# Last layer: sums over slots and the product with adj on VectorE in the gathered buffer, one matmul a block

## What is computed

```python
s = node_feats @ msg_w[:, :D].T
d = node_feats @ msg_w[:, D:].T
messages = gelu(s[:, None, :] + d[None, :, :] + msg_b)
aggregated = einsum('ijd,ij->id', messages, adj)
new_feats = concatenate([node_feats, aggregated]) @ upd_w.T + upd_b
h = gelu(new_feats) + node_feats
return layernorm(h) * ln_w + ln_b
```

## Time and profile before

| | |
|---|---|
| median of three runs | 939.18 us (938.51 to 940.09) |
| the profiled execution, its own time | 940.4 us |
| its span, first to last instruction | 938.7 us |
| TensorE (PE) busy | 685.3 us, 73% |
| GpSimd (POOL) busy | 517.7 us, 55% |
| VectorE (DVE) busy | 426.3 us, 45% |
| ScalarE (ACT) busy | 365.3 us, 39% |

### The profile page before, as it was taken

The page is one execution under the profiler, slowest core; times in us unless marked ns, Lnnn a source line. Parts: engine busy times, 40 slices in busy tenths (PEclk is TensorE's granted clock), DMA queues, the critical chain, the costliest instruction groups (busy, mean ns, idle before and its releaser), DMA issues.

```text
span 938.7 us, 8329 instructions
## 1 busy us (share of the span) xinstructions
PE 685.3 (73%) x2458; PEld 402.5 (43%) x2458; DVE 426.3 (45%) x1529; ACT 365.3 (39%) x591; POOL 517.7 (55%) x513
## 2 busy tenths in 40 slices
PE   1254666999799997989466985285777588589794
PEld 1211142444365644535355633063455356355463
DVE  2298837098986398914435200204413333143222
ACT  0456623468314239654301240134234324442541
POOL 7999199876762067620270067574746656657200
PEclk8669555999879998979655577577979979788685
DMA  8976801799651039930120011111211112111000
GB/s 355 362 283 282 364 1 59 269 409 383 234 186 60 1 133 403 397 150 21 48 60 26 26 40 50 40 50 35 55 32 43 48 37 49 46 45 40 16 6 5
DMA packets 35041, 120.80 MB, mean 129 GB/s; under 512 B 9014, under 2 KB 21748, under 8 KB 25972
## 3 DMA queue, kind: packets, MB, share of 16 engines
...
HBM read 114.66 MB, written 5.55 MB: 128 GB/s over the span
## 4 chain that ended last, share of the span: by engine, by line
PE 44%; DVE 12%; another core or an unknown queue 11%; issue 10%; POOL 8%; DMA 8%; ACT 7%; SPq 0%; POOLq 0%; ACTq 0%
PE ps L114 43%; POOL X L924 8%; DMA ring<-in_adjT_dram 8%; ACT dg L1149 2%; DVE Mh L1744 1%; DVE M L1733 1%; ACT L1158 1%; ACT msg L1158 1%; DVE st L1772 1%; DVE w L1617 1%; DVE w L1619 1%; PE ps L1282 1%; DVE Mh L1732 1%; DVE w L1615 1%
## 5 line engine op out<-in xcount | busy, mean ns | idle before, releaser
L913 POOL DMA_INDIRECT G<-near,IX x176 | 176.5, 1003 | 124.2 <-issue 52.4
L924 POOL TENSOR_TENSOR X<-X,ring 128x2708 f32<-128x2708 f32 (+1 forms) x22 | 129.8, 5902 | 25.9 <-DMA ring<-in_adjT_dram 23.1
L114 PE MATMUL ps<-ring,xT_s 128*128 128x512 f32 (+2 forms) x264 | 114.0, 575 | 8.6 <-DMA ring<-in_adjT_dram 8.6
L114 PE MATMUL ps<-ring,hwu 128*128 128x512 f32 (+3 forms) x264 | 117.0, 597 | 1.0 <-ACT hwu L1016 1.0
L1740 DVE COPY listed<-ps 128x386 f32<-128x386 f32 x11 | 6.2, 560 | 238.6 <-issue 85.6
L114 PE MATMUL ps<-G,ident 128*128 128x512 f32 (+1 forms) x88 | 57.9, 743 | 51.3 <-ACT msg L1158 43.5
L1551 DVE FIND_INDEX8 I<-V,rows 128x8 uint32<-128x340 f32 (+2 forms) x176 | 88.1, 504 | 0.0
L1561 DVE MAX8 V<-rows 128x8 f32<-128x340 f32 (+2 forms) x176 | 85.6, 497 | 0.8
L114 PEld LDWEIGHTS ps<-ring,hwu 128*128 128x128 f32 (+1 forms) x264 | 52.0, 207 | 65.9 <-issue 64.6
L114 PE MATMUL ps<-pd,ident 128*128 128x512 f32 (+3 forms) x116 | 70.1, 701 | 6.9 <-issue 4.9
L1023 ACT ACTIVATE binT<-ring 128x2708 bf16<-128x2708 f32 (+1 forms) x22 | 54.0, 2456 | 44.2 <-PE ps L114 36.0
...
## 6 DMA issues: line engine op xcount, KB each, us to landing
...
G<-near,IX POOLq DMA_INDIRECT x176
...
```

Source lines behind the costliest of these rows:

```text
L114: return pe.matmul(dst, lhsT, rhs, start=start, stop=stop, skip_group_check=True)
L913: pool.indirect_dma_start(out=dst, out_offset=None, in_=table, in_offset=bass.IndirectOffsetOnAxis(ap=index, axis=0), bounds_check=N - 1, ...
L924: pool.tensor_tensor(S[0:rn(j), 0:N], S[0:rn(j), 0:N], ring[0:rn(j), j % RING, :], ALU.add).then_inc(o_S, 1)
```

## The change

- The group loop makes only d. s follows behind the loop for six chunks of four blocks; own_parts on VectorE adds msg_b and writes pd3.
- before_gelu(n) is on VectorE, in G3: it adds s, which own_shares puts in PSUM by an identity product, to the eight slots, and to d of the block itself as a ninth slot. messages(n) takes the gelu of all nine in place. aggregate(n) on VectorE multiplies the nine by T9 (T8 with diag as ninth column) and sums over them; TensorE then adds the block by one identity product that also transposes it. weights and messages_own are gone.
- take_list reads the three groups with six operations instead of ten.
- G3 has room for six blocks; a place is free when VectorE has aggregated its block. A pair's list is gathered before its blocks.
- The gathers have no bound. With it the built program has a register write of 2707 ahead of each of the 231 gathers; without it none.
- lists(1) stands ahead of the group loop, rows_to_list(2) behind it; normal2(0) comes before take_list(1); checks() moves behind pair 1.

The diff, cut to its core:

```diff
-QUEUE3 = 4
+QUEUE3 = 6
...
-        T8 = sb("T8", [P, NB, TOP])
+
+        T9 = sb("T9", [P, NB, TOP + 1])
+        T8, diag = T9[:, :, 0:TOP], T9[:, :, TOP]
...
-        G3 = sb("G3", [P, QUEUE3, TOP, D], life=life)
+        G3 = sb("G3", [P, QUEUE3, TOP + 1, D], life=life)
...
-                                        in_offset=bass.IndirectOffsetOnAxis(ap=index, axis=0),
-                                        bounds_check=N - 1, oob_is_err=False).then_inc(signal, 16)
+                                        in_offset=bass.IndirectOffsetOnAxis(ap=index, axis=0)).then_inc(signal, 16)
...
             for g in range(NG3):
-                for n in (2 * g, 2 * g + 1):
-                    if n >= QUEUE3:
-                        pool.wait_ge(p_pre, 2 * (n - QUEUE3 + 1))
-                    for k in range(TOP):
-                        gather(G3[0:rn(n), n % QUEUE3, k, :], near3[:, :], IX[0:rn(n), n, k:k + 1], s_g[2 * (n % QUEUE3) + k // 4])
                 pool.wait_ge(v_list, g + 1)
                 if g >= 2:
                     pool.wait_ge(p_opre, g - 1)
                 for k in range(CAP):
                     gather(Go[:, g % 2, k, :], near3[:, :], IO[:, g, k:k + 1], s_go[g % 2])
+                for n in (2 * g, 2 * g + 1):
+                    if n >= QUEUE3:
+                        pool.wait_ge(v_agg, n - QUEUE3 + 1)
+                    for k in range(TOP):
+                        gather(G3[0:rn(n), n % QUEUE3, k, :], near3[:, :], IX[0:rn(n), n, k:k + 1], s_g[n % QUEUE3])
...
             def messages(n):
-                r = rn(n)
-                if n >= 2:
-                    act.wait_ge(p_agg, n - 1)
-                for h in range(2):
-                    act.wait_ge(p_pre, 2 * n + h + 1)
-                    act.activation(msg[0:r, n % 2, 4 * h:4 * h + 4, :], bank((2 * n + h) % 3)[0:r, :].rearrange("p (k d) -> p k d", d=D),
-                                   ACT.Gelu).then_inc(c_msg, 1)
+                act.wait_ge(v_pre, n + 1)
+                at = G3[0:rn(n), n % QUEUE3, :, :]
+                act.activation(at, at, ACT.Gelu).then_inc(c_msg, 1)
...
-            def update(g):
-                act.wait_ge(p_sums, g + 1)
...
+            def features(g):
...
+            def deviations3(g):
...
-            weights(0)
-            for q in range(CH):
-                messages_own(q)
-            weights(1)
             for g in range(NG3):
+                messages_listed(g)
                 messages(2 * g)
                 if g:
-                    weights(2 * g + 1)
-                    messages_listed(g - 1)
-                    update(g - 1)
+                    deviations3(g - 1)
                 messages(2 * g + 1)
-                if 2 * g + 2 < NB:
-                    weights(2 * g + 2)
-            messages_listed(NG3 - 1)
-            update(NG3 - 1)
+                aggregated(g)
+                features(g)
+            deviations3(NG3 - 1)
...
                 if g == 0:
                     pe.wait_ge(c_pr, CH)
                     lists(0)
-                if g == 1:
                     lists(1)
...
+            for q in range(CH):
+                if q >= 2:
+                    pe.wait_ge(v_s, q - 1)
+                for i, n in enumerate(blocks_of(q)):
+                    last = mm(pe, bank(6 + q % 2, i * D, D)[0:rn(n), :], x3T[:, n, 0:rn(n)], w3c[:, D:2 * D], True, True)
+                last.then_inc(p_pr, 1)
+
+            def own_shares(g):
+
                 if g >= 2:
-                    pe.wait_ge(c_pr, CH + g - 1)
-                for q, n in enumerate(range(first, first + count)):
-                    at = bank(4 + g % 2, q * D, D)[0:rn(n), :]
...
-                    last = mm(pe, at, ones[0:1, 0:rn(n)], b3_b[0:1, 0:D], False, True)
+                    pe.wait_ge(v_pre, 2 * g - 2)
+                if g < NG3 - 1:
+                    last = mm(pe, bank(g % 2, 0, 2 * D), ident[:, :], pd3[:, 2 * g:2 * g + 2, D:2 * D], True, True)
+                else:
...
+                        n = 2 * g + i
+                        last = mm(pe, bank(g % 2, i * D, D)[0:rn(n), :], ident[0:rn(n), 0:rn(n)], pd3[0:rn(n), n, D:2 * D], True, True)
                 last.then_inc(p_pr, 1)
...
-            def before_gelu(n):
-                r = rn(n)
-                for h in range(2):
-                    if 2 * n + h >= 3:
-                        pe.wait_ge(c_msg, 2 * n + h - 2)
-                    pe.wait_ge(s_g[2 * (n % QUEUE3) + h], past2[2 * (n % QUEUE3) + h] + 64 * (n // QUEUE3 + 1))
-                    at = bank((2 * n + h) % 3)[0:r, :].rearrange("p (k d) -> p k d", d=D)
-                    mm(pe, at, ident[0:r, 0:r], G3[0:r, n % QUEUE3, 4 * h:4 * h + 4, :], True, False)
-                    last = mm(pe, at, ident[0:r, 0:r], pd3[0:r, n, D:2 * D].unsqueeze(1).broadcast_to([r, 4, D]), False, True)
-                    last.then_inc(p_pre, 1)
...
-            def aggregate(n):
...
-                for k in range(TOP):
-                    mm(pe, at, msg[0:r, n % 2, k, :], dg[0:r, n % 2, k, 0:r], n % 2 == 0 and k == 0, False)
-                mm(pe, at, msgd[0:r, n, :], dg[0:r, n % 2, TOP, 0:r], False, False).then_inc(p_agg, 1)
...
+                    pe.wait_ge(c_aggS, g)
...
+            def aggregate(n):
+                r = rn(n)
+                pe.wait_ge(v_agg, n + 1)
+                mm(pe, bank(5, n % 2 * P, r), agg[0:r, n % 2, :], ident[0:r, 0:r], False, n % 2 == 1).then_inc(p_agg, 1)
...
+            pe.wait_ge(v_s, CH)
+            pe.wait_ge(c_d, len(GROUPS2))
+            own_shares(0)
+            own_shares(1)
             for g in range(NG3):
-                before_gelu(2 * g)
-                if g:
-                    aggregate(2 * g - 1)
-                    listed_before_gelu(g - 1)
-                    aggregate_listed(g - 1)
-                    new_features(g - 1)
+                listed_before_gelu(g)
                 if g + 2 < NG3:
                     lists(g + 2)
-                before_gelu(2 * g + 1)
+                aggregate_listed(g)
                 aggregate(2 * g)
-            aggregate(NB - 1)
-            listed_before_gelu(NG3 - 1)
-            aggregate_listed(NG3 - 1)
-            new_features(NG3 - 1)
+                aggregate(2 * g + 1)
+                if g + 2 < NG3:
+                    own_shares(g + 2)
+                new_features(g)
...
-                dve.tensor_copy(listed[:, 0:2, :], bank(7, 0, 2 * EDGE).rearrange("p (k e) -> p k e", e=EDGE))
-                few.done(dve.tensor_copy(listed[:, 2, :], bank(6, 0, EDGE)))
-                for k in range(CAP):
-                    for i, (to, of) in enumerate(((eidx[:, k:k + 1], listed[:, k, 0:w]), (eval_[:, g, k:k + 1], listed[:, k, w:2 * w]))):
-                        dve.scalar_tensor_tensor(out=Mh[:, i, k * w:(k + 1) * w], in0=listed[:, k, 2 * w:3 * w], scalar=ecol[:, k:k + 1], in1=of,
-                                                 op0=ALU.is_equal, op1=ALU.mult, accum_out=to)
+                here, chosen = Mh[:, 0, 0:CAP * w].rearrange("p (k w) -> p k w", w=w), Mh[:, 1, :].rearrange("p (k i w) -> p k i w", i=2, w=w)
+                few.done(dve.tensor_copy(listed[:, :, :], list_bank[:, :, 0:EDGE]))
+                few.done(dve.tensor_tensor(here, listed[:, :, 2 * w:3 * w], ecol[:, :].unsqueeze(2).broadcast_to([P, CAP, w]), ALU.is_equal))
+                few.done(dve.tensor_tensor(chosen, listed[:, :, 0:2 * w].rearrange("p k (i w) -> p k i w", w=w),
+                                           here.unsqueeze(2).broadcast_to([P, CAP, 2, w]), ALU.mult))
+                few.done(dve.tensor_reduce(entry[:, g, :, :], chosen, AX.X, ALU.add))
                 few.done(dve.tensor_copy(erow[:, g, :], listed[:, :, 3 * w]))
-                dve.tensor_copy(IO[:, g, :], eidx[:, :]).then_inc(v_list, 1)
+                dve.tensor_copy(IO[:, g, :], entry[:, g, :, 0]).then_inc(v_list, 1)
...
             for g, (first, count) in enumerate(GROUPS2):
+                normal2(g, first, count)
                 if g == 0:
-                    rows_to_list(2)
-                if g == 1:
                     take_list(1)
-                normal2(g, first, count)
...
+            def own_parts(q):
+
...
+                dve.wait_ge(p_pr, CH + q + 1)
...
+                    last = dve.tensor_tensor(pd3[0:r, n, D:2 * D], bank(6 + q % 2, (first - b[0]) * D, m * D)[0:r, :].rearrange(
+                        "p (q w) -> p q w", w=D), b3_b[0:r, 0:D].unsqueeze(1).broadcast_to([r, m, D]), ALU.add)
+                last.then_inc(v_s, 1)
...
+            def before_gelu(n):
+                r, q = rn(n), n % QUEUE3
+                own = bank(n // 2 % 2, n % 2 * D, D)[0:r, :]
+                dve.wait_ge(p_pr, 2 * CH + n // 2 + 1)
+                dve.tensor_tensor(G3[0:r, q, TOP, :], pd3[0:r, n, 0:D], own, ALU.add)
+                dve.wait_ge(s_g[q], past2[q] + 128 * (n // QUEUE3 + 1))
```

(36 more changed lines are left out.)

91 lines of the change are left out of this document (25 added, 66 removed).

## The result

The changed kernel took 957.2 us (median of four runs, 955.8 to 960.0) against 939.6 for the kernel before: ratio 1.019, 95% interval 1.017 to 1.022. I had forecast 808 us with 0.03 for slower. The profiled execution has a span of 955.2 us. Ratios in this document leave out runs in the slower state of the chip, of which c1_after (823.0 us) and d1_before_group (864.8 us) have one each, so they are not always the quotient of the medians beside them.

The account below looks back on a forecast made before the run. TensorE's own order was taken as the bound. First pair aggregated at 544.8, ten pairs at 24.4, 2 for checks() and a 16.6 tail gave a span of 807.4, so 808 us; range 772 to 836.

Parts of the forecast that it names:

- What bounds the kernel: Last layer's pair loop: TensorE in its own order, with ScalarE's messages between its steps, takes 31.4 us a pair.
- the way round in a pair: Last layer after the change: the chain through VectorE, TensorE and ScalarE sets each pair, 24.4 us at half clock.
- T + 4.6: Pair loop: TensorE ends new_features 4.6 us after VectorE ends aggregating the pair's second block.
- T + 9.0: Pair loop: TensorE ends the listed sums 9.0 us after VectorE ends aggregating the pair's second block.
- Group loop: Ahead of the last layer: each further group of four costs 6.05 us instead of 9.3; first gather 515.7 instead of 543.4.
- My middle: Gathers without the bound: 1.15 us each, taken between 1.00 (whole gap goes) and 1.30 (nothing gained).
- The lock-out by VectorE's product: Pair loop: a gather beside VectorE's product of two SBUF inputs waits; 0.7 us a block, 1.4 a pair.
- The reduction: VectorE's strided sum over a block's 1152 elements: 1.35 us, with bounds 1.35 and, at half rate, 2.7.
- my two cases: TensorE's clock in the pair loop: half clock, 24.4 us a pair (taken), or full clock, 20.2.
- 0.75 and more wherever wide products stand: TensorE's granted clock, argued for the rival of full clock and cheap gathers: 760 to 790 us, chance 0.19.
- the rival in which the bound was free and gathers decide: Last layer: gathers stay at 1.30 us, 24.8 a pair; kernel 813 us, up to 830; chance 0.18.
- the one rival for that, VectorE locking out gathers: Pair loop: busy VectorE locks out each gather; 939 us reached at 37 us a pair, 1.96 a gather; chance 0.03.

Follow-up runs that it names:

- c1_after: The changed kernel itself, nothing altered, in a session where the kernel before takes about 860 us: 814.4 us, ratio 0.938.
- d1_before_group: The kernel before with only the new group loop (second projection behind it, list steps moved): first gather at 518.3, only 8 us gained at the end.
- d4_before_look: The kernel before, nothing altered, run for its trace in a session where it takes about 860 us instead of about 940.
- d2_reduce_in_line: The changed kernel with the reduction reading its elements in the order they lie, without the stride: 814 us, a reduction 1352 ns instead of 2086.
- e2_half_gathers: The changed kernel with only four of eight gathers a block from the seventh block on: 23.9 us a pair; no kernel time given.
- f2: The changed kernel with 400 small DMAs added and GpSimd waiting for TensorE's listed sums ahead of each pair's block gathers: 871 us.
- f1: The changed kernel with 400 small DMAs from SyncE added in the pair loop, without any added GpSimd wait: 952 us.
- h1: The changed kernel with added GpSimd waits for TensorE in both layers' gathers, and three more in the first two pairs: 855.9 us.
- h2: The changed kernel itself, nothing altered, measured again in the session of the kernel with most added waits: 949.8 us.
- g3_before_pause: The kernel before with GpSimd waiting, ahead of each pair's block gathers, until TensorE has added up block 2g-3: 939.0 us.

## Why the prediction was wrong

**What bounds the kernel.** I took all of the 31.4 us a pair for TensorE's work in its own order, because it was busy 76%. In d4_before_look the same order takes 27.3. The mechanism was right for the most part, and 4 of the 31.4 us were something else: on record TensorE was busy 23.9 us a pair at a granted clock of 0.82, where d4_before_look has 20.8 at 0.89 (667.12 to 816.69, with 552 matmuls recorded instead of 576), and ScalarE waited 7.9 to 8.6 us "remote" ahead of `dg` in every second pair, where d4_before_look has 2.4 to 2.5 ended by TensorE. The sign was in the earlier trace rows: 43.5 and 24.8 us of ScalarE that end "remote". I read only idle times with a named releaser. Not every such wait is a sign, though: VectorE waits 16.6 us a pair for its list in d4_before_look as well, there with TensorE named.

**The step that failed** is the way round in a pair, 24.4 us. There ScalarE copies new_features at T + 4.6 and takes the listed sums at T + 9.0, as soon as TensorE has made them. On record, in the pair shown, it copied new_features 4.9 us and took the listed sums 23.5 us after TensorE's records of them end, every second pair was held up in this way, and a pair took 36.3 us on average. Against c1_after, where nothing is late, the first gather came 10.8 us later, the gathers took 362.9 us instead of 267.7, and from the last gather to the end it was 63.9 us instead of 28.4.

**Group loop.** The 6.05 us a group were 6.11 in c1_after (copies of `x3T` there start at 489.32 and 495.43), the first gather 517.6 against 515.7. On record it was 528.4, 10.8 later than in c1_after, where the two idle times together are 12.3 us shorter.

**Gathers.** 1.25 us, not 1.15: leaving out the bound shortened the instruction by 0.05, and the 0.30 gap did not go. My middle was wrong, the upper bound nearly right. The lock-out by VectorE's product is real but was over-sized. Two products of c1_after, and three gathers beside them:

```profile
682.55 1.36 DVE L1787 TENSOR_TENSOR G<-G,T 128x1152 f32<-128x1152 f32 x1 [0.50 <-ACT G L1124]
707.11 1.34 DVE L1787 TENSOR_TENSOR G<-G,T 128x1152 f32<-128x1152 f32 x1
```
```profile
682.71 2.02 POOL L910 DMA_INDIRECT G<-near,IX  x1 [0.30 <-issue]
706.59 0.94 POOL L910 DMA_INDIRECT G<-near,IX  x1 [0.30 <-issue]
707.84 1.43 POOL L910 DMA_INDIRECT G<-near,IX  x1 [0.30 <-issue]
```

The gathers that start inside a product, at 682.71 and 707.84, both end 2.2 us after the product's start, as if they had begun about when it ended; so do all 19 of c1_after that start between 0.1 and 1.2 us into a product (2.1 to 2.2). But most start just before a product or in its last 0.3 us, where it costs them 0.1 us or nothing. So of all 176 block gathers on record the mean is 969 against a median of 947 ns, 0.4 us a pair and not 1.4. The Trainium skill (SBUF — State Buffer, Who interferes with whom) infers that a product of two SBUF tensors does not hold up descriptor writing; these rows speak against it.

**VectorE.** The product was right (1.36 for 1.35). The reduction was under-sized: 2.09 instead of 1.35, near the middle of my bounds. The Trainium skill (SBUF — State Buffer, Specifications) states that SBUF has lines of 16 bytes, that two accesses to a line are needed for full bandwidth and that each cross to a new line costs; I had not weighed it. A stride of 128 elements does that each time, and d2_reduce_in_line agrees. The time of the kernel did not hang on it.

**Way round and clock.** Without late signals the way round is 23.9 us (e2_half_gathers) against 24.4; the granted clock in the stretch of the gathers is 0.65 in c1_after and 0.61 on record, between my two cases. My "0.75 and more wherever wide products stand" was already not so in the earlier trace rows, which has 0.67 from 880 us on.

**Sum and rivals.** Where signals are not late, the kernel takes 814.4 us: inside the range, 6 us above the forecast, and at the value of the rival in which the bound was free and gathers decide (813). That number is partly luck: I had the kernel before at 31.4 us a pair, and where nothing is late the pairs go from 27.3 to 24.6. On record the kernel was slower, and the one rival for that, VectorE locking out gathers, is not the reason; the reason stood in no rival. Why the old order met it less is argued, not shown: its GpSimd stood still 3 to 8 us once or twice a pair, waiting for TensorE, while six buffers instead of four and the list gathers ahead of the blocks let two pairs run on end. The way round then closed a ring: the second pair's late signals hold back ScalarE's messages, these VectorE, this the next list, and GpSimd stands still for 24 us until that list comes. That GpSimd's waits take the long pairs away is shown for the changed kernel (f2 against f1, h1 against h2, each in one session). That it is the unbroken gathering they end, and not that GpSimd runs two pairs ahead of TensorE, is argued: the test that keeps the lead and thins the gathers, e2_half_gathers, fell in a session without late signals. For the kernel before g3_before_pause speaks against it.

**What stays open.** Why some sessions have the late signals and others not, and where on its way a signal is held. In f2_more_signals_pause a cluster of twelve counts of SyncE's small DMAs is recorded within 698.8 to 699.1 us, when the gathers had stopped, with about ten in the 15 us before, so TensorE's signals may not be the only ones held. And the traces of these sessions lack most records of landings in the last layer (on record 79 to 123 in 50 us between 550 and 800 us, in c1_after 528 to 698) and many of the engines' own signals (10 to 68 against 59 to 98), while up to 460 us both kinds have as many. Missing records and late engines come together, and every run listed has a span and a granted clock, so each was recorded by the profiler. That the recording itself holds up the engines is a rival that no run here tests; a time taken without it would. The Trainium skill (SBUF — State Buffer, Who interferes with whom) says that TensorE and ScalarE never wait on anyone and that DMA never contends with a compute engine; that is said of SBUF's ports, and these rows show a coupling of GpSimd's gathers and the moment at which TensorE's work is seen, which is of another kind.
